# Scan layer: two of sixteen products on GpSimd by way of ScalarE's copies, and the residual added by a matmul

## The reference, cut to what matters

```python
xi, z = split(gn(x) @ W_in)
xc = silu(causal_conv4(xi) + conv_b)          # 64 channels d
dt_r, B, C = split(xc @ W_x)                  # 2 + 16 + 16
dt = softplus(dt_r @ W_dt + b_dt)
h[d,s] = exp(dt[d] * A[d,s]) * h[d,s] + dt[d] * B[s] * xc[d]      # per step of t
y[d] = sum_s h[d,s] * C[s]
out = x + ((y + xc * D_skip) * silu(z)) @ W_out
```

## Time and profile before

| | |
|---|---|
| median of 3 runs (lowest, highest) | 3547.14 us (3538.5, 3556.32) |
| the profiled execution | 3545.76 us |
| its span | 3543.9 us |
| first scan starts at, last starts at | 1685.59 us, 3529.91 us |
| VectorE busy in 2000 to 3400 us | 1378.92 of 1400 us |
| ScalarE, GpSimd, TensorE busy there | 1002.29, 1151.35, 1192.45 us |

### The profile page before, as it was taken

The page is one execution under the profiler, slowest core; times in us unless marked ns, Lnnn a source line. Parts: engine busy times, 40 slices in busy tenths (PEclk is TensorE's granted clock), DMA queues, the critical chain, the costliest instruction groups (busy, mean ns, idle before and its releaser), DMA issues.

```text
span 3543.9 us, 39955 instructions
## 1 busy us (share of the span) xinstructions
PE 2714.6 (77%) x12330; PEld 806.7 (23%) x12330; DVE 2515.5 (71%) x2216; ACT 1902.1 (54%) x2335; POOL 1992.6 (56%) x1228
## 2 busy tenths in 40 slices
PE   3766887667878658753888888888888888888886
PEld 1122212222222223111222222222222222222221
DVE  3433554434554335322999999999999999999998
ACT  1412464313455113433767676777777676767672
POOL 1232413313323325112787878888887878787886
PEclk9877998868999679876999999999999999999998
DMA  5566631658513668454767676676767676767664
GB/s 120 123 192 201 195 90 48 160 171 241 138 56 94 176 180 248 117 113 90 177 147 170 151 165 157 154 168 144 177 142 175 143 174 148 171 149 165 156 160 110
DMA packets 284502, 536.59 MB, mean 151 GB/s; under 512 B 70681, under 2 KB 173409, under 8 KB 283873
## 3 DMA queue, kind: packets, MB, share of 16 engines
q1 hardware_dynamic: 251456, 453.97, 51.8%
q0 software_dynamic: 16128, 55.06, 5.8%
q10 hardware_dynamic: 16800, 26.07, 3.0%
HBM read 396.31 MB, written 138.65 MB: 151 GB/s over the span
## 4 chain that ended last, share of the span: by engine, by line
issue 17%; DVE 15%; PE 14%; ACT 3%; DMA 2%; POOL 1%; ACTq 1%; DVEq 0%; POOLq 0%; SPq 0%
DVE m_pb L420 10%; PE m_pb L270 4%; DVE m_hs L425 4%; PE m_py L253 4%; PE m_misc L218 2%; PE m_misc L237 1%; DMA m_dtb<-dt_rows 1%; ACT m_da L377 1%; PE m_py L249 1%; DMA dt_rows<-m_dt 1%; DVE m_gated L407 1%; PE m_misc L224 1%; ACT m_xg L300 1%; POOL m_hs L451 0%; DVE m_fin L435 0%
## 5 line engine op out<-in xcount | busy, mean ns | idle before, releaser
L451 POOL TENSOR_TENSOR m_hs<-m_hs,m_cs 128x1024 f32<-128x1024 f32 x512 | 1205.4, 2359 | 346.2 <-DVE m_hs L425 346.2
L425 DVE TENSOR_TENSOR_SCAN m_hs<-m_da,m_pb 128x1024 f32<-128x1024 f32 x512 | 1170.8, 2287 | 33.0 <-ACT m_da L377 6.3
L270 PE MATMUL m_pb<-m_dtx,late 64*128 64x512 f32 x2048 | 597.4, 649 | 219.2 <-DVE m_hs L425 218.6
L377 ACT ACTIVATE m_da<-m_dtb,m_a_neg 128x1020 f32<-128x1020 f32 x512 | 579.5, 1143 | 287.1 <-DMA m_dtb<-dt_rows 210.6
L420 DVE TENSOR_TENSOR m_pb<-m_pb,m_bs 128x1024 f32<-128x1024 f32 x512 | 620.5, 1212 | 34.5 <-PE m_pb L270 34.0
L253 PE MATMUL m_py<-m_hs,late 128*64 128x512 f32 x2048 | 566.6, 632 | 60.4 <-POOL m_hs L451 60.4
L1382 POOL TENSOR_TENSOR t_xc<-t_xc,big 128x512 f32<-128x512 f32 x96 | 119.2, 1265 | 382.0 <-DVE big L1318 382.0
L1190 ACT ACTIVATE t_sq<-t_bank 128x512 f32<-128x512 f32 x192 | 106.6, 595 | 415.5 <-PE t_bank L1056 415.2
L1344 POOL DMA_DIRECT2D late<-right_factor x96 | 57.0, 594 | 466.4 <-PE t_bank L991 254.3
L1202 ACT ACTIVATE t_gate<-t_bank,t_small 128x512 f32<-128x512 f32 x192 | 122.1, 684 | 354.8 <-PE t_bank L1000 342.0
L991 PE MATMUL t_bank<-late,t_lwin 128*128 128x256 f32 x816 | 237.6, 430 | 95.7 <-DMA late<-right_factor 61.0
(11 more groups left out here) (150 smaller groups left out, 3690.4 us busy)
## 6 DMA issues: line engine op xcount, KB each, us to landing
m_dtb<-dt_rows SPq DMA_DIRECT2D x512, 512.0 KB, 6.1
right_factor<-t_tile SPq DMA_DIRECT2D x384, 128.0 KB, 2.4
late<-right_factor POOLq DMA_DIRECT2D x96, 512.0 KB, 6.0
t_tile<-band_out SPq DMA_DIRECT2D x384, 128.0 KB, 2.8
band_out<-t_vwin SPq DMA_DIRECT2D x48, 496.0 KB
band_out<-t_vwin SPq DMA_DIRECT2D x48, 480.0 KB
dt_rows<-m_dt ACTq DMA_DIRECT2D x64, 256.0 KB, 3.3
t_xc<-in_x_cm SPq DMA_DIRECT2D x16, 512.0 KB, 20.5
```

The costliest lines, as they stand in the source:

```text
L270: m = nc.tensor.matmul(pb[s % 2][:, half(n)], spread[rows, dg, :], dtx[par][rows, half(q)], start=True, stop=True)
L377: nc.scalar.activation(da[:, s % DA_RING, :, 1:T], dtb[s % DTB_RING][:, :].rearrange("p (r t) -> p r t", t=T)[:, :, 1:T], ACT.Exp, scale=a ...
L425: nc.vector.tensor_tensor_scan(hs[:, s % H_RING, :], da[:, s % DA_RING, :, :].rearrange("p r t -> p (r t)"), pb[s % 2][:, :], 0.0, ALU.mul ...
L451: nc.gpsimd.tensor_tensor(hs[:, s % H_RING, :], hs[:, s % H_RING, :], cs[q][:, :], ALU.mult).then_inc(hc_ready, 1)
```

## The change

Steps 3 and 11 (`APART`, one of each half) are taken out of the common way. Their spread dt*x goes into `misc` (TensorE, op `u0` or `u1`), ScalarE copies it to a new buffer `ub` in SBUF, GpSimd multiplies it by `bs`, and ScalarE copies the product (1024 elements) into `pb`, where VectorE's scan reads it. VectorE has no product in these steps. The other 14 steps (`INLINE`) stay as they were. `u1` (for step 11 of the same chunk) is made by TensorE behind step 3, copied behind 4 and multiplied by GpSimd behind 6; `u0` (for step 3 of the next chunk) is made behind 13, copied behind 14 ahead of the stores and of `dt_rows`, and multiplied behind 15. The copy back into `pb` stands at the head of ScalarE's step 4 and 12. Besides, `fin` is no sum on VectorE any more: a matmul with an identity matrix adds x in `py[1]`, and ScalarE copies the result to `fin` behind step 9.

```diff
+    APART = (3, 11)
+    INLINE = [s for s in range(S) if s not in APART]
...
         SHARES = {
-            "tensor": {0: [(PRE, "x")], 2: [(OWN, "bq1")], 4: [(OWN, "cq1")], 5: [(PRE, "dt")], 8: [(PRE, "z")],
-                       7: [(POST, "out")], 9: [(PRE, "bq0")], 11: [(PRE, "cq0")]},
+            "tensor": {0: [(PRE, "x")], 2: [(OWN, "bq1")], 3: [(OWN, "u1")], 4: [(OWN, "cq1")], 5: [(PRE, "dt")], 8: [(PRE, "z")],
+                       7: [(POST, "out")], 9: [(PRE, "bq0")], 11: [(PRE, "cq0")],
+                       13: [(PRE, "u0")]},
...
-                       8: [(PRE, "sp_back"), (PRE, "sp_relu")], 9: [(PRE, "silu_z")], 10: [(PRE, "bq0")], 12: [(PRE, "cq0")],
-                       13: [(NEXT2, "xg0")], 14: [(POST, "store"), (PRE, "dt_rows")], 15: [(NEXT2, "xg1")]},
-            "vector": {4: [(POST, "gate1")], 8: [(POST, "out")], 11: [(OWN, "gate0")]},
-            "gpsimd": {7: [(PRE, "loss0"), (PRE, "log0")], 8: [(PRE, "dt0"), (PRE, "loss1")],
+                       8: [(PRE, "sp_back"), (PRE, "sp_relu")], 9: [(POST, "fin"), (PRE, "silu_z")], 10: [(PRE, "bq0")], 12: [(PRE, "cq0")],
+                       13: [(NEXT2, "xg0")], 14: [(PRE, "u0"), (POST, "store"), (PRE, "dt_rows")], 15: [(NEXT2, "xg1")]},
+            "vector": {4: [(POST, "gate1")], 11: [(OWN, "gate0")]},
+            "gpsimd": {6: [(OWN, "u1")], 15: [(PRE, "u0")], 7: [(PRE, "loss0"), (PRE, "log0")], 8: [(PRE, "dt0"), (PRE, "loss1")],
...
+                    elif op in ("u0", "u1"):
+                        q = int(op[1])
+                        pe.wait_ge(dtx_ready, 2 * k + q + 1)
+                        for n in range(2):
+                            rows = slice(D * n, D * n + D)
+                            pe.wait_ge(misc_used[n], use(k, op))
+                            nc.tensor.matmul(misc[n][:, :], spread[rows, APART[q] % DG, :], dtx[par][rows, half(q)],
+                                             start=True, stop=True).then_inc(misc_ready[n], 1)
...
+                    nc.tensor.matmul(py[1][:, :], eye[:, :], xm[:, :, bass.ds(SUB * k, SUB)].rearrange("p t n -> p n t"),
+                                     start=True, stop=False, skip_group_check=True)
...
+                    elif op in ("u0", "u1"):
+                        q = int(op[1])
+                        for n in range(2):
+                            a.wait_ge(misc_ready[n], use(k, op) + 1)
+                            nc.scalar.copy(ub[q][:, half(n)], misc[n][:, :]).then_inc(misc_used[n], 1)
...
                 def steps(k, par, s, first, last):
+                    if s - 1 in APART:
+                        q = APART.index(s - 1)
+                        a.wait_ge(u_made[q], k + 1)
+                        a.wait_ge(h_ready, S * k + s - 2)
+                        nc.scalar.copy(pb[(s - 1) % 2][:, :], ub[q][:, :]).then_inc(u_back[q], 1)
...
+                    if op[:-1] == "u":
+                        for n in range(2):
+                            g_.wait_ge(misc_used[n], use(k, op) + 1)
+                        nc.gpsimd.tensor_tensor(ub[q][:, :], ub[q][:, :], bs[q][:, :], ALU.mult).then_inc(u_made[q], 1)
```

More of the change, by code:

```diff
@@ L48, in mamba_layer @@
         gn_bias = sb("gn_bias", [P, 1])
-        (avg, w_in, conv_w, w_z, wx_dt, w_dt, w_bc, w_out, w_skip, vecs, a_log, spread, gather) = (t for t, _ in shared.weights)
+        (avg, w_in, conv_w, w_z, wx_dt, w_dt, w_bc, w_out, w_skip, vecs, a_log, spread, gather, eye) = (t for t, _ in shared.weights)
         w_conv = sb("w_conv", [P, TAPS // 2, P])
@@ L65, in mamba_layer @@
         dtb = [sb(f"dtb{i}", [P, W]) for i in range(DTB_RING)]
+        ub = [sb(f"ub{i}", [P, W]) for i in range(2)]
         da = sb("da", [P, DA_RING, 2 * SUB, T])
@@ L136, in mamba_layer @@
         dt_stored = [sem(f"dt_stored{i}") for i in range(2)]
+        u_made, u_back = ([sem(f"{n}{i}") for i in range(2)] for n in ("u_made", "u_back"))
         dtb_loaded = [sem(f"dtb_loaded{i}") for i in range(DTB_RING)]
@@ L142, in early @@
             return isinstance(k, int) and k < n
[L144 to L145 removed]
+        FIRST_USE = {"x": 0, "dt": 1, "z": 2, "bq0": 3, "cq0": 4, "u0": 5}
+        USE = {"x": 0, "bq1": 1, "u1": 2, "cq1": 3, "dt": 4, "z": 5, "bq0": 6, "cq0": 7, "u0": 8}
+        OWN_USE = ("bq1", "u1", "cq1")
         def use(k, name):
@@ L149, in use, with inline @@
                 return FIRST_USE[name]
-            body = k if name in ("bq1", "cq1") else k - 1
+            body = k if name in OWN_USE else k - 1
             if isinstance(k, int) and body == CHUNKS - 1:
-                return len(FIRST_USE) + len(USE) * body + ("bq1", "cq1").index(name)
+                return len(FIRST_USE) + len(USE) * body + OWN_USE.index(name)
             return len(FIRST_USE) + len(USE) * body + USE[name]
+        def inline(k, s):
+            return len(INLINE) * k + INLINE.index(s) + 1
         def stores_of(k, par):
@@ L265, in steps @@
                         pe.wait_ge(dtx_ready, 2 * k + q + 1)
[L266 to L272, removed]
+                    if s in INLINE:
+                        if not (first and s < 2):
+                            pe.wait_ge(h_ready, g - 1)
+                        for n in range(2):
+                            rows = slice(D * n, D * n + D)
+                            m = nc.tensor.matmul(pb[s % 2][:, half(n)], spread[rows, dg, :], dtx[par][rows, half(q)],
+                                                 start=True, stop=True)
+                        m.then_inc(b_ready, 1)
                     if s >= LAG:
@@ L361, in pre @@
                         nc.scalar.activation(sp_x[:, :], sp_x[:, :], ACT.Relu).then_inc(sp_relu, 1)
+                    elif op in ("u0", "u1"):
[3 more added lines that the diff above has]
+                            nc.scalar.copy(ub[q][:, half(n)], misc[n][:, :]).then_inc(misc_used[n], 1)
                     else:
-                        dst, busy = ((bs, u_done), (cs, hc_ready))["bc".index(op[0])]
+                        dst, busy, per = ((bs, u_done, len(INLINE)), (cs, hc_ready, S))["bc".index(op[0])]
                         q = int(op[2])
                         if not early(k, 1):
-                            a.wait_ge(busy, S * k if q else S * k - DG)
+                            a.wait_ge(busy, per * k if q else per * k - per // 2)
                         for n in range(2):
@@ L389, in post @@
                 def post(k, par, op):
+                    if op == "fin":
+                        a.wait_ge(o_ready, k + 1)
+                        if not early(k, 1):
+                            a.wait_ge(stored, 16 * G * k)
+                        nc.scalar.copy(fin[:, :], py[1][:, :]).then_inc(fin_done, 1)
+                        return
                     a.wait_ge(fin_done, k + 1)
@@ L418, in steps @@
                         v.wait_ge(misc_used[1], use(k, f"bq{q}") + 1)
-                    v.wait_ge(b_ready, g + 1)
-                    nc.vector.tensor_tensor(pb[s % 2][:, :], pb[s % 2][:, :], bs[q][:, :], ALU.mult).then_inc(u_done, 1)
-                    v.wait_ge(u_done, g + 1)
+                    if s in INLINE:
+                        v.wait_ge(b_ready, inline(k, s))
+                        nc.vector.tensor_tensor(pb[s % 2][:, :], pb[s % 2][:, :], bs[q][:, :], ALU.mult).then_inc(u_done, 1)
+                        v.wait_ge(u_done, inline(k, s))
+                    else:
+                        v.wait_ge(u_back[q], k + 1)
                     v.wait_ge(da_ready, g + 1)
@@ L428, in post @@
                 def post(k, par, op):
[L429 to L438, removed]
+                    gate(k, par, 1)
                 schedule(v, "vector", pre, steps, post)
@@ L457, in pre @@
                     cols = half(q)
-                    if op[:-1] == "loss":
+                    if op[:-1] == "u":
+                        for n in range(2):
+                            g_.wait_ge(misc_used[n], use(k, op) + 1)
+                        nc.gpsimd.tensor_tensor(ub[q][:, :], ub[q][:, :], bs[q][:, :], ALU.mult).then_inc(u_made[q], 1)
+                    elif op[:-1] == "loss":
                         g_.wait_ge(sp_act_done, k + 1)
@@ L1464, in _layout @@
             spread[:, g, d, g, :, d] = 1
+    a["eye"] = np.eye(P, dtype=np.float32)
     a["spread"] = spread.reshape(P, 8, P)
@@ L1481, in __init__ @@
                                    ("w_skip", P, (P,)), ("vecs", P, (2,)), ("a_log", P, (8,)), ("spread", P, (8, P)),
-                                   ("gather", P, (8, HID))):
+                                   ("gather", P, (8, HID)), ("eye", P, (P,))):
             size = shape[0] * (shape[1] if len(shape) > 1 else 1)
```

4 lines of the change are left out of this document (2 added, 2 removed).

## The result

The changed kernel took 3794.79 us (median of 4 runs, 3793.51 to 3798.92) against 3548.05 us before in the same runs: a ratio of 1.0698, 95% interval 1.067 to 1.0727. The forecast was slower by 153 us; it is slower by 247 us, and 3794.79 lies above the range. The direction and the path were right; what the low clock costs was put far too low, and VectorE's own stretch was half a microsecond a chunk too short.

A forecast was written before the change was run, and what follows sets the result against it. The prediction took VectorE to bound the kernel and a cross-engine loop of 62.4 us a chunk to replace it: 3545.8 us plus 143 for the loop and 15 for the clock gave 3704, so 3700 us, range 3590 to 3765.

The forecast's parts named there:

- VectorE's bound would be lost to a loop through dtx0, u0, dt_rows and decay 0': Likeliest case, chance 0.72: this loop across the chunk boundary takes 62.4 us, 4.7 more than now.
- The rival by the Trainium skill's queue depth: ScalarE's queue of 8 lets dt_rows issue before u0 has landed: 57.5 us a chunk, 3540 us; chance 0.12.
- Term 1: GpSimd from the end of scan 6: products 6 to 10, u1 and seven half pieces, 23.0 us.
- Terms 4 and 5: dt_rows' write and read until decay 0' is released, 8.0 us; then decay 0' and both xg1 halves, 3.75 us.
- Terms 2 and 3: TensorE's u0 with handover, 1.2 us; then ScalarE's four stores and the second dt_rows, 2.8 us.
- the term of the clock: TensorE at 1.2 GHz after idling before the convolution's second half: 0.5 us a chunk (bounds 0 and 2.9), 15 us.
- term 6: TensorE's second half of the convolution and spread 1', up to product 1': 3.3 us.
- Term 7: VectorE from product 1' to the end of scan 6', less the product of step 3: 20.4 us.
- VectorE-bound: Rival: VectorE stays the bound, so 106 us go and the kernel takes 3440 us; chance 0.08.
- The unheld case: Rival: dt_rows isn't held behind u0; a GpSimd and convolution loop binds at 57.5 us, 3540 us; chance 0.12.
- The dearer case: Rival: low clock or dear copy back worsens the convolution or VectorE's stretch, 3778 us; chance 0.08.
- The identity matmul: TensorE behind step 7, reading x at a 1 KB stride: 1.1 us taken, bounds 1.1 and 2.7, up to 2 covered.

The follow-up runs named there:

- the hold alone: Kernel before plus one wait: ScalarE waits for dtx0 ahead of the stores and dt_rows, no work added; 3678.34 us, ratio 1.0362.
- u0 alone: Changed kernel without u1: only step 3 is taken out, step 11 is as before, fin by the matmul stays; 3759.89 us, ratio 1.0599.
- u1 early: Changed kernel with GpSimd's u1 product behind step 5 instead of 6; 3763.14 us, ratio 1.0623.
- The fillers: Changed kernel plus matmuls whose result is overwritten: ahead of u0 and the convolution's second half 3800.7 us; ahead of the second half alone 3725.22 us, ratio 1.0508.
- mended: Changed kernel with stores and dt_rows ahead of u0's copies, u1 behind step 5, VectorE's wait for the product last; 3513.49 us, ratio 0.9903.
- dt_rows first: Changed kernel with ScalarE's stores and dt_rows ahead of the copies of u0 behind step 14; 3559.38 us, ratio 1.0054.

## Why the prediction was right in kind and wrong in size

- *VectorE's bound would be lost to a loop through dtx0, u0, dt_rows and decay 0'*: shown three ways, by adding the hold alone (+134 us), by taking it out (-235 us) and by u0 alone (+215 us).
- *The sequencer doesn't pass an unmet wait*: shown. In the changed kernel the first store issues at 2594.11, 0.2 us after the first u0 copy starts, although its own condition (fin, copied at 2572.15) was met long before. The rival by the Trainium skill's queue depth (Advanced Engine Details and Errata, "Engine Queue Depths") is out: whatever waits in the page's queue of 8 instructions, DMAs behind it did not issue.
- *Term 1, 23.0 us*: 22.87. Right as summed. What the rivals' part says, that u1 moves the pieces 2.32 us back, was not: without u1 product 7 waits for scan 7, so u1 costs 1.05 us, as the runs with u0 alone and with u1 early show.
- *Terms 4 and 5* (8.0 and 3.75): 8.04 and 3.69.
- *Terms 2 and 3* (4.0 to dt_rows 2): 5.05. TensorE stood idle for 2.74 us, then ran sum 10 and u0; u0 ran at the low clock (0.50), 2.08 instead of 1.13 us. I had weighed the clock only for the convolution. Where u0 took 1.13, the stretch to dt_rows 1 was 3.47 us, as forecast.
- **The step that failed is the term of the clock**, taken as 0.5 us of 0 to 2.9 for term 6 and as nothing for u0. The stretch to product 1' was 5.36 us instead of 3.3, and u0 added 1.0: 3 us a chunk, some 92 us, not 15. The fillers gave back 70 of them. "The first microsecond after such a gap is mostly at full speed" was read from one group that stood behind 2.28 us of idle time; here 5 us went before instead of the forecast's 3 to 4, and the second half of the convolution was slow from its first record on (3.57 us). A longer idle time isn't needed for that: with the hold alone, 2.84 us went before, and it took 3.58.
- *Term 7, 20.4*: 20.93. A scan starts up to 0.16 us later behind its product, which comes with a count of products that differs from the steps'; 0.06 of it goes with the order of the waits, the rest is open. I had taken waits on a free engine as free.
- The sum: 62.4 + 0.5 was forecast; 62.4 with 2.1 and 1.0 for the clock and 0.5 for the gaps is 66.0; less 0.1 for term 1 it is 65.9, the sum of the medians, against a mean chunk of 65.77.
- *Rivals*: VectorE-bound was wrong by 355 us, and even mended the kernel doesn't get there (56.65 us, not 54.3). The unheld case, 57.5 us a chunk and 3540 us, is the kernel with dt_rows first: 57.97 and 3559. The number is luck, for the loop that binds there runs through u0 and spread 14, which the rival left out. The dearer case, 3778, was the nearest number to the result, and I gave it 0.08.
- *The identity matmul*: the stride is 256 bytes, 64 columns of 4 bytes, not the 1 KB of the prediction; ScalarE's reads of x, from which its upper bound was made, have the same stride. It took 1.96 us against 1.12 for L266 with the same weights' shape and contiguous data, a factor 1.75, both at a granted clock of 1.00. The stride is the likely cause; no run has the same matmul on contiguous data. The Trainium skill's cacheline note (SBUF — State Buffer, "Door 1: The DMA port swizzle") agrees in kind. It was covered, as said: without it the kernel took 3789.13 us.

## What to carry to other kernels

Work moved off the bounding engine has to be followed to every queue that it is put into: here two copies ahead of two DMA issues on ScalarE cost more than the 106 us that they were to free, and putting them behind, with the same work on every engine, brought the loss from 7% down to 0.5%; with two more orders mended it was a gain of 1%. Before an operation with a wait goes into a queue, look for what stands behind it whose result takes long to come back, and let that go first. If a forecast makes TensorE stand idle for some microseconds ahead of matmuls on the path, count those at the low clock. And when a loop is taken away, look anew at which step the bounding engine waits for: a chunk time that fits the next loop on the list doesn't show that it is this loop.

## What I had not expected of the hardware

- The second half of the convolution ran at half speed (3.38 to 3.78 us instead of 1.99) in all 25 chunks of the changed kernel, after 4.6 to 6.0 us without matmuls. With the hold alone, after 2.1 to 3.3 us, it did so in 21 of 25 chunks (3.11 to 3.79) and took 1.99 in the other four, so the length of the idle time alone doesn't tell. With fillers and 0.4 to 1.7 us left it took 1.99 in all. Fillers help only within the idle time; behind it they run at the low clock and delay what follows (3.78 us for two).
- Where the product's count differs from the step's, a scan starts 1.40 us behind the product's start instead of 1.24. With the wait for the product last among three it is 1.34.
- Two costs came out where the rows or the lower bound had them: GpSimd's products took 2358 ns beside VectorE's (2359), and ScalarE's copy of 1024 elements from SBUF into PSUM 1026 ns.
